# Causal block kernel: the second normalisation of batches 1 to 3 moved from the prologue into rounds 0 to 9, and statistics rewritten

## What is computed

```python
mod = (silu(c) @ wmod).reshape(4, 6, 1, -1)
sa, ca, ga, sb, cb, gb = (mod[:, k] for k in range(6))
ga, gb = clipped_away_from_zero(ga), clipped_away_from_zero(gb)      # |.| at least 0.25, sign kept
h = layernorm(x) * (1 + ca) + sa
x = x + ga * plain_attention(h)               # one head of 128, not causal, softmax over 1024 keys
h = layernorm(x) * (1 + cb) + sb              # the second normalisation
x = x + gb * ffn(h)

def ffn(h):
    r = h + causal_attention(rmsnorm(h, g1))  # 16 query heads of 64, 4 key heads, rotary
    return r + top2_of_8_experts(rmsnorm(r, g2))
```

## Time and profile before

| | us |
|---|---|
| median of 3 runs (1346.33 to 1348.85) | 1348.4 |
| the profiled execution, device time | 1348.97 |
| its span, first to last instruction | 1347.1 |
| PE busy in the span | 1122.7 |
| DVE busy | 1058.7 |
| POOL busy | 1004.5 |
| ACT busy | 881.7 |

### The profile page before, as it was taken

The page is one execution under the profiler, slowest core; times in us unless marked ns, Lnnn a source line. Parts: engine busy times, 40 slices in busy tenths (PEclk is TensorE's granted clock), DMA queues, the critical chain, the costliest instruction groups (busy, mean ns, idle before and its releaser), DMA issues.

```text
span 1347.1 us, 36055 instructions
## 1 busy us (share of the span) xinstructions
PE 1122.7 (83%) x14984; PEld 841.0 (62%) x14984; DVE 1058.7 (79%) x2177; ACT 881.7 (65%) x1508; POOL 1004.5 (75%) x786
## 2 busy tenths in 40 slices
PE   4879885499999999999999999999999997600990
PEld 2768673256766767677676776676767776500880
DVE  6588767688888988889889888898888975592665
ACT  3656573478888878888788887787888894100330
POOL 2645876589988889879898898888987996226454
PEclk9889996699999999999999999999999999555996
DMA  6240010221212212112121121221211200022783
GB/s 215 51 136 2 2 63 24 74 79 52 60 55 61 47 54 68 45 51 57 45 75 37 52 61 55 60 49 52 75 38 25 61 3 2 0 91 72 221 291 140
DMA packets 49247, 90.85 MB, mean 67 GB/s; under 512 B 8896, under 2 KB 19136, under 8 KB 48832
## 3 DMA queue, kind: packets, MB, share of 16 engines
q1 hardware_dynamic: 46128, 81.21, 21.2%
q0 software_dynamic: 2960, 7.38, 2.1%
HBM read 43.96 MB, written 13.01 MB: 42 GB/s over the span
## 4 chain that ended last, share of the span: by engine, by line
PE 62%; DVE 20%; POOL 6%; issue 4%; ACT 3%; SPq 2%; DMA 2%; POOLq 0%; DVEq 0%; ACTq 0%
PE psS L1164 5%; PE psT L1094 5%; PE psS L1163 5%; PE psT L1082 5%; PE psS L1185 5%; PE psS L1186 5%; PE psS L1187 5%; PE psT L1112 3%; PE psO L1094 3%; PE psO L1164 3%; PE psO L1163 3%; POOL rows_in L716 2%; DVE pmax L1571 2%; DVE psT L1548 2%; DVE arena L1550 2%
## 5 line engine op out<-in xcount | busy, mean ns | idle before, releaser
L690 POOL TENSOR_TENSOR probs<-arena,probs 128x512 f16<-128x512 f32 x576 | 656.5, 1157 | 109.7 <-ACT probs L878 104.3
L878 ACT ACTIVATE probs<-arena 128x512 f16<-128x512 f32 x576 | 361.4, 627 | 14.8
L1185 PE MATMUL psS<-vb,probs 128*128 128x65 f16 x2304 | 302.0, 193 | 3.1 <-POOL probs L690 0.8
L1186 PE MATMUL psS<-vb,probs 128*128 128x64 f16 x2304 | 303.6, 194 | 0.0
L1187 PE MATMUL psS<-vb,probs 128*128 128x65 f16 x2304 | 301.5, 192 | 0.0
L890 ACT ACTIVATE arena<-psS 128x512 f32<-128x512 f32 x384 | 225.7, 588 | 106.0 <-PE psS L1167 64.1
L1185 PEld LDWEIGHTS psS<-vb,probs 128*128 128x128 f16 x2304 | 220.2, 97 | 70.9 <-issue 9.8
L1186 PEld LDWEIGHTS psS<-vb,probs 128*128 128x128 f16 x2304 | 215.5, 97 | 47.4
L1571 DVE TENSOR_REDUCE pmax<-psT 128x1 f32<-128x512 f32 (+1 forms) x305 | 193.6, 639 | 39.5 <-PE psT L1094 18.9
L1187 PEld LDWEIGHTS psS<-vb,probs 128*128 128x128 f16 x2304 | 216.9, 98 | 0.0
L1571 DVE TENSOR_REDUCE pmax<-psO 128x1 f32<-128x512 f32 (+1 forms) x207 | 139.3, 673 | 24.5 <-PE psO L1094 16.9
(11 more groups left out here) (269 smaller groups left out, 2887.3 us busy)
## 6 DMA issues: line engine op xcount, KB each, us to landing
arena<-arena SPq DMA_DIRECT2D x240, 128.0 KB, 2.4
arena<-w_exp_dram SPq DMA_DIRECT2D x40, 384.0 KB, 4.3
arena<-xnT_d SPq DMA_DIRECT2D x16, 512.0 KB, 3.6
wkv<-w_d SPq DMA_DIRECT2D x16, 352.0 KB, 4.0
rows_in<-arena POOLq DMA_DIRECT2D x1, 2580.0 KB, 21.2
arena<-rows_in SPq DMA_DIRECT2D x40, 64.5 KB, 3.2
arena<-x_dram SPq DMA_DIRECT2D x4, 512.0 KB, 5.2
hres<-x_dram SPq DMA_DIRECT2D x4, 512.0 KB, 5.3
```

Of the source, the lines that this page charges most:

```text
L690: pool.tensor_tensor(pl[:, r, :], pf[:, r, :], ph[:, r, :], ALU.subtract).then_inc(lo_P, 1)
L878: act.activation(ph[:, s % RING, :], pf[:, s % RING, :], ACT.Copy).then_inc(b_hi, 1)
L1185: pe.matmul(dst, high, vb[:, p, j, 0:OW], start=first, stop=False, skip_group_check=True)
L1186: pe.matmul(dst[:, 0:HD], high, vb[:, p, j, HD + 2:VW], start=False, stop=False, skip_group_check=True)
```

## The change

The second normalisation of batch 1 from its second variance on, of batch 2 from its first variance on and of batch 3 as a whole leave the prologue. Tables by round and step (`NORM_V`, `NORM_A`, `NORM_P`, `OUT_AT`) put its instructions behind fixed steps of rounds 0 to 8 on DVE, ACT and POOL. What turns the batch's features is a new kind of side entry, `in2`, two of them for each batch (`INPUT_AT`, rounds 0, 1, 4, 5, 8, 9): 4 transposes on PE, the high half on ACT straight from PSUM, the low half on DVE. POOL's `input2_low` of these batches is gone, and ACT's second pass over the rows. DVE's products over a batch are halved there (`a_centre`, `c`). SP stores a batch at the end of round 1, 5 or 9 and waits in `load_round` for the batch's store; a load of round 4 is issued in round 2.

The statistics change for both normalisations: the mean's tensor_scalar goes, its factor is in the centring, now a scalar_tensor_tensor; the variance's tensor_scalar becomes a scalar_tensor_tensor that adds a tile of epsilons, `epsb`, which two new memsets fill. Batches 2 and 3 are centred into hres in place of n2, and their squares lie in a tile of their own.

```diff
+INPUT_AT = {0: {29: (1, 0)}, 1: {31: (1, 1)}, 4: {29: (2, 0)}, 5: {31: (2, 1)}, 8: {33: (3, 0)}, 9: {29: (3, 1)}}
+
+NORM_V = {0: {4: ("d", 1)}, 1: {4: ("b", 2)}, 2: {4: ("c", 2, 0), 13: ("c", 2, 1)}, 3: {24: ("d", 2)},
+          6: {4: ("a", 3), 11: ("a_centre", 3, 0), 17: ("a_centre", 3, 1), 28: ("b", 3)},
+          7: {4: ("c", 3, 0), 13: ("c", 3, 1)}, 8: {14: ("d", 3)}}
+NORM_A = {3: {16: ("squares", 2, 1)}, 6: {22: ("squares", 3, 0)}, 8: {8: ("squares", 3, 1)}}
+NORM_P = {0: {7: ("power", 1, 1)}, 1: {8: ("power", 2, 0)}, 2: {18: ("scaled", 2)}, 3: {8: ("shifted", 2), 30: ("power", 2, 1)},
+          5: {8: ("gated", 3), 30: ("with_rows", 3)}, 6: {32: ("power", 3, 0)}, 7: {18: ("scaled", 3), 32: ("shifted", 3)},
+          8: {18: ("power", 3, 1)}}
+OUT_AT = {(0, s): (1, s - 12) for s in range(12, 20)} | {(4, s): (2, s - 8) for s in range(8, 16)} | {
+    (8, s): (3, s - 22) for s in range(22, 30)}
...
+        if s in INPUT_AT.get(it, {}):
+            now.append(("in2",) + INPUT_AT[it][s])
...
             def load_round(it, p):
 
+                sp.wait_ge(xn_out, 16 * (it // HKV) + 16)
...
-            norm2_power(1, 1)
-            norm2_power(2, 0)
-            gated(3)
-            with_rows(3)
-            pool.wait_ge(xsum, B)
+            pool.wait_ge(a_x1, 2 * B)
             pool.memset(kB[HD:HD + 1, :, :], 1.0).then_inc(ones_set, 1)
...
+                    if s in NORM_P.get(it, {}):
+                        norm2(*NORM_P[it][s])
...
+            def input2_high(e, bank, full):
+
+                c, h = e[1:]
+                act.wait_ge(side_full, full)
+                if c > 1:
+                    act.wait_ge(xn_out, 16 * c)
+                act.activation(xhl_late[:, 0, :].rearrange("d (p j) -> d p j", j=NT)[:, :, 4 * h:4 * h + 4],
+                               side_banks[bank].rearrange("d (j p) -> d p j", p=P), ACT.Copy, scale=g1T[:, 0:1]
+                               ).then_inc(xn_hi, 1)
...
+                if kind == "in2":
+                    pe.wait_ge(n2_out, 1 + NT * e[1])
+                    for j in range(4):
+                        mm = pe.transpose(dst[:, j * P:(j + 1) * P], n2s_late[:, 4 * e[2] + j, :], ident)
+                    return mm
...
-                if PROLOGUE[i] == ("q", 0, 0):
-                    pe.wait_ge(a_E, NL)
-                    turn_input2(1, psS[:, 0, :])
                 if PROLOGUE[i] == ("max", G, 0):
-                    turn_input2(2, psS[:, 1, :])
                     pe.wait_ge(ones_set, 4)
-                if PROLOGUE[i] == ("max", G + 1, 0):
-                    pe.wait_ge(n2_T, 2)
-                    turn_input2(3, psS[:, 0, :])
...
                 if part == 0:
                     v.tensor_reduce(st[:, 0, :], src, AX.X, ALU.add).then_inc(n, 1)
-                    v.wait_ge(n, at + 1)
-                    v.tensor_scalar(st[:, 1, :], st[:, 0, :], -1.0 / D, None, ALU.mult).then_inc(n, 1)
-                else:
-                    v.wait_ge(n, at + 2)
-                    v.tensor_tensor(dst, src, bc_tok(st[:, 1, :]), ALU.add).then_inc(n, 1)
-
-            def variance(n, at, sq, st, eps):
-
-                v.tensor_reduce(st[:, 2, :], sq, AX.X, ALU.add).then_inc(n, 1)
-                v.wait_ge(n, at + 1)
-                v.tensor_scalar(st[:, 3, :], st[:, 2, :], 1.0 / D, eps, ALU.mult, ALU.add).then_inc(n, 1)
+                    return
+                v.wait_ge(n, per * c + 1)
+                ins = v.scalar_tensor_tensor(dst[:, cut, :], bc_tok(st[:, 0, :])[:, cut, :], -1.0 / D, src[:, cut, :],
+                                             ALU.mult, ALU.add)
+                if cut.stop == NT:
+                    ins.then_inc(n, 1)
+
+            def variance(n, sq, st, eps):
+
+                v.tensor_reduce(st[:, 2, :], sq, AX.X, ALU.add).then_inc(own_sum, 1)
+                own_sums[0] += 1
+                v.wait_ge(own_sum, own_sums[0])
+                v.scalar_tensor_tensor(st[:, 3, :], st[:, 2, :], 1.0 / D, epsb[:, eps, :], ALU.mult, ALU.add).then_inc(n, 1)
...
+                elif kind == "in2":
+                    c, h = e[1:]
+                    v.wait_ge(xn_hi, 2 * (c - 1) + h + 2)
+                    high, low = (xhl_late[:, a, :].rearrange("d (p j) -> d p j", j=NT)[:, :, 4 * h:4 * h + 4] for a in range(2))
+                    ins = v.scalar_tensor_tensor(low, src.rearrange("d (j p) -> d p j", p=P), g1T[:, 0:1], high,
+                                                 ALU.mult, ALU.subtract)
...
-                if e == ("k", 1):
-                    norm2_a(3)
-                if e == ("r", 0, 0):
-                    norm2_b(3)
-                if e == ("r", 0, 1):
-                    norm2_c(3)
-                if e == ("v",):
-                    norm2_d(2)
-                if e == ("r", 1, 1):
-                    norm2_d(3)
...
+                    if s in NORM_V.get(it, {}):
+                        norm2(*NORM_V[it][s])
```

More of the change, by code:

```diff
@@ L68 @@
 ROW_AT = 5
-READER = {"max": "V", "row": "A", "k": "V", "v": "V", "q": "V", "r": "V", "turn": "V", "out": "V", "gap": "-"}
+READER = {"max": "V", "row": "A", "k": "V", "v": "V", "q": "V", "r": "V", "turn": "V", "out": "V", "in2": "V", "gap": "-"}
 def reader(entry):
@@ L123, in start @@
 def start(it, eng=None):
-    if isinstance(it, int) and it == 0:
-        return count(PROLOGUE, eng)
-    if isinstance(it, int) and it == NKV:
-        return start(NKV - 1, eng) + count(flat(side_work(False, True)), eng)
-    return it * count(flat(side_work(False, False)), eng) + (
-        count(PROLOGUE, eng) + count(flat(side_work(True, False)), eng) - count(flat(side_work(False, False)), eng))
-assert all(len(w) % SB == 0 for w in (PROLOGUE, flat(side_work(True, False)), flat(side_work(False, False)),
-                                      flat(side_work(False, True))))
+    return count(PROLOGUE, eng) + sum(count(flat(side_work(r)), eng) for r in range(it))
+assert all(len(w) % SB == 0 for w in [PROLOGUE] + [flat(side_work(r)) for r in range(NKV)])
 NL = B * NT
@@ L498, in round_loads @@
                     load_round(it + 2, p)
-                work = [e for e in flat(side_work(first, last)) if reader(e) == "A"]
+                work = [e for e in flat(side_work(it)) if reader(e) == "A"]
                 def row_of(h):
@@ L513, in round_loads @@
                     spread_row(row_of(4), 1 - p, 0)
+                for c, h in INPUT_AT.get(it, {}).values():
+                    if h == 1:
+                        store_input2(c, it)
             round_loads(0, 0, True, False, True)
@@ L840, in _, with vec_read_of @@
                     input2(b - 3, psTf)
-            VEC_AT = {e: i for i, e in enumerate(x for x in flat(side_work(False, False)) if reader(x) == "V")}
-            VEC_FIRST = {e: i for i, e in enumerate(x for x in flat(side_work(True, False)) if reader(x) == "V")}
-            VEC_PRO = {e: i for i, e in enumerate(x for x in PROLOGUE if reader(x) == "V")}
+            def vec_read_of(it, e):
+                work = PROLOGUE if it < 0 else flat(side_work(it))
+                own = [x for x in work if reader(x) == "V"].index(e)
+                return own if it < 0 else start(it, "V") + own
             def high_half(c, n, p, read_at):
@@ L880, in act_round @@
             def act_round(it, p, first, last):
-                steps = side_work(first, last)
+                steps = side_work(it)
                 work = flat(steps)
@@ L892, in act_round @@
                         c = HIGH_AT[s]
-                        high_half(c, it + 1, 1 - p, start(it, "V") + (VEC_FIRST if first else VEC_AT)[ROTATED[c]])
+                        high_half(c, it + 1, 1 - p, vec_read_of(it, ROTATED[c]))
                     for e in steps[s]:
@@ L896, in act_round @@
                             read(e, i % SB, start(it) + count(work[:i + 1]), 1 - p)
+                        if e[0] == "in2":
+                            input2_high(e, i % SB, start(it) + count(work[:i + 1]))
                         i += 1
+                    if s in NORM_A.get(it, {}):
+                        norm2_squares(*NORM_A[it][s][1:])
+                    if (it, s) in OUT_AT:
+                        norm2_late(*OUT_AT[it, s])
             for i, e in enumerate(PROLOGUE):
@@ L1611, in _, with norm2 @@
                     own += 1
[L1612 to L1621 removed]
+            def norm2(op, c, h=0):
+                half = slice(4 * h, 4 * h + 4)
+                if op == "a":
+                    norm2_a(c, 0)
+                elif op == "a_centre":
+                    norm2_a(c, 1, half)
+                elif op == "b":
+                    norm2_b(c)
+                elif op == "c":
+                    norm2_c(c, half)
+                else:
+                    norm2_d(c)
             def vec_round(it, p, first, last):
[L1624 removed]
+                steps = side_work(it)
                 work = flat(steps)
                 i, own = 0, 0
+                if it == 1:
+                    v.wait_ge(n2_s, 4)
```

154 lines of the change are left out of this document (78 added, 76 removed).

## The result

| us | before | after |
|---|---|---|
| median (4 runs each on this chip) | 1347.62 | 1324.91 (1322.86 to 1326.71) |
| profiled execution | 1348.97 | 1324.32 |
| its span | 1347.1 | 1322.5 |

The account below looks back on a forecast made before the run. The prologue was taken as a chain of hand-overs with no engine full, the rounds as bound by PE. Prologue -29, stage A -1.5, DVE +10, `in2` +5.4, ACT +3.5 give -11.6 on 1348.97: 1337, range 1325 to 1347.

Parts of the forecast that it names:

- Direction and prologue: Whole kernel faster; between projected rows and first scores, the chain without the second normalisation's work gains 29 us.
- Stage A: Stage up to the last projected rows: centrings without their tensor_scalar gain 1.5 us, ends 0 and 3.
- rival 4: New centrings run at half speed, five on the first stage's chain at 1.2 us more each: 1343, chance 0.06.
- ACT, PE, POOL, SP: Rounds' cost on engines other than DVE: 5.4 us for six `in2`, 3.5 for ACT, nothing for POOL and SP.
- 0.9 on each `in2`: Rounds: PE's share and part of DVE's wait for each of six `in2` entries, 5.4 us in all.
- a third of ACT's time: Rounds: of 10.5 us of scaled copies and squarings, a third falls where ACT is waited for: 3.5 us.
- DVE's 10 us: Rounds 0 to 8: moved DVE instructions, with waits for POOL, less the delay each place bears: 10 us together.
- At most 1.2: Rounds: a DVE instruction waits for POOL's next change of instruction, 0.5 us on the mean, at most 1.2.
- Rival 2: Rounds: DVE comes in only when POOL pauses, eleven instructions wait 4 us longer each, 44 in all: 1381, chance 0.08.
- 3 us and above: Rounds: DVE's two-input products should take 0.7 to 1.9 us; 3 us and above would show waiting for POOL's pauses.
- Rival 1: Rounds make up DVE's delays; transposes and some 4 us remain, 8 instead of 19: 1327, chance 0.24.
- 17 and 6: Rounds, upper end for DVE: each instruction paid whole (17 us) and a mean wait for all eleven (6), given as 24.

Follow-up runs that it names:

- experiment 5: The kernel before with the new statistics alone, nothing moved: 1341.0 us, ratio 0.9947.
- experiment 7: Changed kernel plus odd-step DVE probes (rounds 10, 14), ACT copies (11), ACT squaring (12), DVE half-batch sum (13): +8.96, +7.35, +0.2, 0.0, 0.0 us.
- experiments 3: Changed kernel plus 16 short DVE probes in each of rounds 10 to 14, behind even steps: +5.05, +5.05, +0.05 (sums), +5.08, +5.04 us.
- experiment 6: Changed kernel plus one DVE sum of known length in each of rounds 10 to 13, two in 14: +0.50, +0.65, +1.04, +0.01, +1.64 us.

## Why the prediction was wrong

- **Direction and prologue: right.** -29.1 against -29. PE starts on the first scores 26.9 us after the projected rows (237.27), where 27.0 were forecast. Inside it, most fills were faster than taken, and the transfer that spreads q was the path that decides.
- **Stage A: under-sized.** -3.1 against -1.5, at the far one of its ends. Its last low half on POOL comes 1.9 us earlier (206.11 for 207.96), which experiment 5 shows to be the statistics' own. The rest, 1.2, is the clock behind it, which the sum had no term for: the 36 matmuls that took 2.37 us at 1.00 in the changed kernel took 3.60 before. The rule that the new centring runs at half speed (rival 4; the Trainium skill, Vector Engine (DVE) Microarchitecture Reference, "Points that are easy to get wrong") falls: over a whole batch it takes 1.22 us where nothing is in its way, as the tensor_tensor before it.

```profile
207.96:213.47 5.51, 3.60 (x36) 3.09 (x36) 3.17 (x8) 2.16 (x9) 1.65 (x2) 0.57 0.00 0
```

```profile
24.84 1.22 DVE L1376 SCALAR_TENSOR_TENSOR arena<-st,arena 128x1024 f32<-128x1024 f32 x1
```

- **The step that failed is "ACT, PE, POOL, SP".** It put 0.9 on each `in2` and a third of ACT's time on top, 8.9 together; the runs show next to nothing of it. The rounds with an `in2` alone (5 and 9) changed by +0.05 and -0.31, the one with eight copies besides (4) by +0.46, and the ACT work of experiment 7 cost 0.2 and 0. In rounds 0, 1 and 8, which have an `in2` beside a variance, it can't be read by itself; there all of it came to 3.0, where DVE's part alone was forecast at 3.5. So some 8 of the 13 us are this term. DVE did wait for ACT in `in2`, 4.5 us before five of them (idle time of DVE by what ended it), but at places where it had that time.

```profile
  ACT O L889: 4.5, 5
```

- **DVE's 10 us: right in sum, by two errors.** Without round 3 the DVE places were over-sized: forecast 8.2 (`in2` apart), measured 3.4 with their `in2` and copies. The half products came in at once (0.68 to 0.72 where 1.2 was taken; round 6's two half centrings took 0.91 and 1.23), and step 4 bears more. In round 3 the forecast was 1.8 and 7.2 came. "At most 1.2" of wait is the sentence that fell there: DVE need not come in at POOL's next change.
- **Rival 2 was near the mechanism, at the wrong frequency.** It said that eleven instructions wait until POOL pauses. One of them lost several turns, at 4.37 us (3 us and above was to be its sign), and it did end with POOL's run; but the waits of 2.65 and 3.83 in experiments 3 and 7 ended while POOL ran on, so a pause isn't needed. Its evidence against (rows 6, DVE between two instructions of POOL) was one case, and experiments 3 and 7 show that both happen. Rival 1's 8 us in the rounds and its time are nearest in number, but by luck: its reason, that delays are made up, is refuted by experiment 6.
- **Two sums are off by one.** Rival 1's own terms (8 us in place of 19) give 1326 and not 1327, and 17 and 6, the upper end of DVE's part, are 23 and not 24. The forecast doesn't hang on either.
- **Behind round 15** the code is the same, and 2.8 us went, all of it behind the router's matmuls (171.1 us from their end to the end of the span before, 168.1 after). It isn't the change's work by any path that I could find, and the experiments' kernels show -1.0 to -8.1 there. This part stays open.

Of the 13 us by which the sum missed, the rounds are 8.2, the stages behind them 3.3 and stage A 1.6.

## What to carry to other kernels

A short DVE instruction of a form that waits for POOL doesn't cost its own length: here it waited 0.5 us on the mean and 2 to 4.4 at single places, and what it then cost depended on what stood behind it. Where POOL runs back to back, do small scaling with immediates on POOL itself, or in a form that doesn't wait (a sum), and put what must wait behind a step that bears the whole of it. Margins (how much delay a place bears), read as "end of the read to start of the next fill of that bank" held to 0.1 to 0.35 us, and work for an engine with 10 us of slack in a round cost nearly nothing; a pause of PE may have to be charged for the clock behind it as well.
